# Reordering ScalarE and VectorE in a two-layer conditioned feed-forward kernel on one Trainium2 core

## The reference

```python
y = einsum('bij,bkj->bik', x, L0_cond_weight[itok_B_1_14])
h = layernorm(y, gamma, beta)
h = quant_rows(h) @ quant_rows(w1).T + b1      # scale = max|row| / 127
h = gelu(h)
h = quant_rows(h) @ quant_rows(w3).T + b3
x = x + h
```

## Time and profile before

| what | us |
|---|---|
| time, median of 3 runs | 810.48 |
| lowest and highest of them | 808.19, 811.26 |
| the profiled execution: time | 810.76 |
| its span, first to last instruction | 809.0 |
| TensorE busy | 740.0 |
| VectorE busy | 523.9 |
| ScalarE busy | 350.1 |
| GpSimd busy | 68.4 |

### The profile page before, as it was taken

The page is one execution under the profiler, slowest core; times in us unless marked ns, Lnnn a source line. Parts: engine busy times, 40 slices in busy tenths (PEclk is TensorE's granted clock), DMA queues, the critical chain, the costliest instruction groups (busy, mean ns, idle before and its releaser), DMA issues.

```text
span 809.0 us, 9935 instructions
## 1 busy us (share of the span) xinstructions
PE 740.0 (91%) x3128; PEld 471.7 (58%) x3128; DVE 523.9 (65%) x1911; ACT 350.1 (43%) x660; POOL 68.4 (8%) x40
## 2 busy tenths in 40 slices
PE   8988999999899999999999799998999995799927
PEld 4544544254444444444666688887878774467616
DVE  4548482426664929365775524225988988999985
ACT  1252633213624333341644635435344252599613
POOL 0002000202630203021004000000000000000000
PEclk9999999999999999999999999999999999799958
DMA  7959954213729443534032133032030328666306
GB/s 304 409 164 404 277 202 153 94 53 130 260 95 390 142 159 138 182 118 156 1 111 87 53 117 118 1 118 108 11 118 17 103 96 285 216 228 200 122 0 208
DMA packets 54278, 124.31 MB, mean 154 GB/s; under 512 B 8015, under 2 KB 33743, under 8 KB 48722
## 3 DMA queue, kind: packets, MB, share of 16 engines
q1 hardware_dynamic: 52930, 120.94, 42.8%
q10 hardware_dynamic: 1296, 2.74, 0.9%
HBM read 98.47 MB, written 25.19 MB: 153 GB/s over the span
## 4 chain that ended last, share of the span: by engine, by line
PE 61%; DVE 17%; ACT 8%; DMA 7%; issue 4%; SPq 1%; POOL 1%; ACTq 0%; DVEq 0%
PE PS L850 17%; PE PS L1021 13%; PE PS L910 13%; DMA stage<-w_dram 3%; DMA wscale_scratch<-wsc 3%; PE PS L899 2%; PE PS L1133 2%; PE PS L1127 2%; PE PS L1173 2%; DVE xp L1422 2%; PE PS L943 2%; PE PS L1055 2%; DVE kprod L1512 2%; PE PS L1142 1%; DVE ksum L1516 1%
## 5 line engine op out<-in xcount | busy, mean ns | idle before, releaser
L850 PE MATMUL PS<-w_raw,x_raw 128*128 128x512 f32 x512 | 230.2, 603 | 5.2 <-DMA w_raw<-cond_w_dram 2.2
L850 PEld LDWEIGHTS PS<-w_raw,x_raw 128*128 128x128 f32 x512 | 96.6, 194 | 116.1 <-issue 114.1
L1021 PE MATMUL PS<-w_hi,xT_hi 128*128 128x512 f32 x256 | 102.7, 401 | 0.0
L1021 PE MATMUL PS<-w_hi,xT_lo 128*128 128x512 f32 x256 | 100.1, 391 | 0.0
L1021 PE MATMUL PS<-w_lo,xT_hi 128*128 128x512 f32 x256 | 100.0, 391 | 0.0
L569 ACT ACTIVATE qT<-PS,round_c 128x512 bf16<-128x512 f32 x64 | 40.2, 679 | 86.5 <-PE PS L899 86.5
L1273 DVE SCALAR_TENSOR_TENSOR gbuf<-PS,lnst,vecs 128x512 f32<-128x512 f32 x32 | 23.9, 750 | 80.2 <-PE PS L910 80.1
L488 POOL TENSOR_TENSOR xres<-xres,vecs 128x1024 f32<-128x1024 f32 x16 | 43.2, 2718 | 305.5 <-DMA xres<-x_tok_dram 305.5
L1516 DVE TENSOR_REDUCE ksum<-kprod 128x16 f32<-128x64 f32 x392 | 66.3, 211 | 0.0
L910 PE MATMUL PS<-w3q,qT 128*128 128x512 bf16 x256 | 58.0, 379 | 6.7 <-ACT qT L569 6.7
L1340 DVE TENSOR_TENSOR xT_lo<-PS,xT_hi 128x512 fp32r<-128x512 f32 x32 | 20.5, 682 | 63.3 <-ACT xT_hi L629 63.2
(11 more groups left out here) (180 smaller groups left out, 1188.4 us busy)
## 6 DMA issues: line engine op xcount, KB each, us to landing
w_raw<-cond_w_dram SPq DMA_DIRECT2D x31, 1024.0 KB, 5.9
x_raw<-x_tr_dram SPq DMA_DIRECT2D x32, 256.0 KB, 6.7
stage<-w_dram SPq DMA_DIRECT2D x16, 512.0 KB, 12.6
xres<-x_tok_dram SPq DMA_DIRECT2D x8, 1024.0 KB, 9.2
x_scratch<-x1buf SPq DMA_DIRECT2D x16, 512.0 KB, 6.6
x1n<-x_scratch SPq DMA_DIRECT2D x16, 512.0 KB, 5.8
y_scratch<-y SPq DMA_DIRECT2D x16, 512.0 KB, 3.7
stage<-base_w_nat_dram SPq DMA_DIRECT2D x8, 512.0 KB, 13.0
```

The costliest lines, as they stand in the source:

```text
L850: mm = pe.matmul(PS[:, 2 * t + h, :], x_raw[pr][:, c, t * P:(t + 1) * P], w_raw[pr][:, c, h * H2:(h + 1) * H2], start=(pr == 0 and c == 0) ...
L1021: pe.matmul(PS[:, 2 * t + h, :], xx[:, c, t * P:(t + 1) * P], ws[c // 2][:, c % 2, h * H2:(h + 1) * H2], start=(c == 0 and xx is xT_hi and ...
```

## The change

Six edits. (1) In the last part of a step s below 7, ScalarE evacuates the GELU transposes of tile 0 (`evac_T(s - 1, 0, 3)`) before the GELU of tile 1, and no more at the head of the next step; the root of the next batch's tile 0 follows that GELU at once, before `quant2`. In the third step `evac_T(1, 0, 3)` stands behind `composites_1`; after step 1 it stands behind the GELU. (2) In `step_a` the evacuation of tile 1 (`evac_T(s - 2, 1, 3)`) moves in front of `ln_root(s - 1, 1)`, and `split_hi(2)` moves behind `quant1`. (3) On VectorE `centre` of the next batch's tile 0 stands in front of `range_w1` of tile 1. (4) On TensorE the block `l0(1, 2)` stands in front of the transposes of stage 12, which go to the T banks now; their evacuation stands behind `quant1(0, 1)`. (5) The waits for free banks follow. (6) `WARM` is 28, not 16.

```diff
--- before.py
+++ after.py
@@ -79,8 +79,8 @@
 
         PS = ctx.enter_context(nc.psum_tensor("PS", [P, 8, H2], F32))
         T_BANK, O_BANK, LL_BANK, LG_BANK = 4, 6, 6, 7
-        WARM = 16
-        IN_O = (1, 3, 5, 7, 9, 11, 12)
+        WARM = 28
+        IN_O = (1, 3, 5, 7, 9, 11)
 
         def stage_bank(m):
 
@@ -591,9 +591,9 @@
             evac_stage(KC + 3)
             quant1(0, 0)
             evac_T(0, 0, 1)
-            evac_stage(KC + 4)
             ln_root(0, 1)
             quant1(0, 1)
+            evac_stage(KC + 4)
             evac_T(0, 1, 1)
             gelu(0, 0)
             quant2(0, 0)
@@ -603,6 +603,7 @@
             evac_stage(KC + 6)
             evac_stage(KC + 7)
             gelu(0, 1)
+            evac_T(0, 0, 3)
             quant2(0, 1)
             act.dma_start(w24[:, :, :], head_w).then_inc(misc_ld, 16)
             act.dma_start(bcol[:, :], bias_col).then_inc(misc_ld, 16)
@@ -630,19 +631,15 @@
                                          PS[:, T_BANK + h, :].rearrange("p (c n) -> p c n", c=4), ACT.Copy).then_inc(xh_done, 1)
 
             def step_a(s):
-                if s == 3:
-                    composites_1()
-                ln_root(s - 1, 0)
-                evac_T(s - 2, 0, 3)
+                if s == 2:
+                    ln_root(s - 1, 0)
+                quant1(s - 1, 0)
                 if s == HALF:
                     split_hi(2)
-                quant1(s - 1, 0)
                 if s == 3:
                     composites_2()
-                    evac_T(s - 2, 1, 3)
+                evac_T(s - 2, 1, 3)
                 ln_root(s - 1, 1)
-                if s != 3:
-                    evac_T(s - 2, 1, 3)
                 quant1(s - 1, 1)
                 if s == HALF:
                     split_hi(3)
@@ -661,7 +658,16 @@
                 if s == NB - 1:
                     evac_xT(0, 1)
                     return
+                if s == 2:
+                    gelu(s - 1, 1)
+                    ln_root(s, 0)
+                    quant2(s - 1, 1)
+                    composites_1()
+                    evac_T(s - 1, 0, 3)
+                    return
+                evac_T(s - 1, 0, 3)
                 gelu(s - 1, 1)
+                ln_root(s, 0)
                 quant2(s - 1, 1)
 
             for s in range(2, NB):
@@ -855,8 +861,10 @@
             def stage_T(m):
                 pe.wait_ge(st_q, m + 1)
                 for h in range(2):
-                    if m <= KC + 4:
-                        wait(pe, st_ev, 2 * (m - (1 if m == KC + 4 else 2)) + h + 1)
+                    if m < KC + 4:
+                        wait(pe, st_ev, 2 * (m - 2) + h + 1)
+                    elif m == KC + 4:
+                        pe.wait_ge(e1_done, h + 1)
                     elif m == KC + 5:
                         pe.wait_ge(e1_done, 2 + h + 1)
                     else:
@@ -869,6 +877,8 @@
             def t_bank_free(s, t, which, h):
                 if which == 1 and s == 0 and t == 0:
                     pe.wait_ge(st_ev, 2 * (KC + 2) + h + 1)
+                elif which == 1 and s == 0:
+                    pe.wait_ge(st_ev, 2 * (KC + 4) + h + 1)
                 elif which == 3 and s == 0 and t == 0:
                     pe.wait_ge(st_ev, 2 * (KC + 7) + h + 1)
                 elif which == 3 and s == NB - 2 and t == 0:
@@ -884,7 +894,7 @@
                 if t == 1:
                     pe.wait_ge(o1_done if which == 1 else o3_done, 4 * s + h + 1)
                 elif which == 1 and s == 0:
-                    pe.wait_ge(st_ev, 2 * (KC + 4) + h + 1)
+                    pe.wait_ge(st_ev, 2 * (KC + 3) + h + 1)
                 elif which == 1:
                     wait(pe, o3_done, 4 * (s - 1) + 2 + h + 1)
                 else:
@@ -924,8 +934,8 @@
             stage_T(KC + 3)
             l0(1, 1)
             transposes(0, 0, 1)
+            l0(1, 2)
             stage_T(KC + 4)
-            l0(1, 2)
             product(0, 0, 1)
             transposes(0, 1, 1)
             l0(1, 3)
@@ -1342,7 +1352,9 @@
                                             xT_hi[:, 4 * h:4 * h + 4, t * P:(t + 1) * P], ALU.subtract).then_inc(xl_done, 1)
 
             def step_a(s):
-                layer_norm(s - 1, 0)
+                if s == 2:
+                    centre(s - 1, 0)
+                normalise(s - 1, 0)
                 if s == 2:
                     dve.wait_ge(swld, 32)
                 if s == 3:
@@ -1352,7 +1364,9 @@
                 finish_w3(s - 2, 1)
                 finish_w1(s - 1, 0)
                 if s < NB - 1:
-                    finish_w1(s - 1, 1)
+                    scale_w1(s - 1, 1)
+                    centre(s, 0)
+                    range_w1(s - 1, 1)
 
             for s in range(2, NB):
                 step_a(s)
```

## The result

| what | before | after |
|---|---|---|
| median of the first comparison (6 executions each) | 809.83 | 801.30 |
| lowest and highest of them | 807.63, 811.26 | 799.25, 803.79 |
| the profiled execution: time, span | 810.76, 809.0 | 803.07, 801.2 |
| all executions of this study: number, mean, median | 72, 809.3, 809.6 | 20, 802.9, 803.3 |

The ratio of the first comparison is 0.9899 (95% interval 0.9873 to 0.9926), that is 8.2 us faster. Two later comparisons of the same kernel gave 0.9915 (0.9884 to 0.9945) and 0.9921 (0.9894 to 0.9948), and the difference of the means over all executions is 6.4 us.

What follows compares the result with a forecast made beforehand. TensorE, busy 740.0 us, was taken as the bound. 810.76 less 2.4 (lead left after step 4) and 3.1 (steps 5 to 7) gave 805.3, forecast as 805.0 since the median is 0.28 lower; 8-in-10 range 802.0 to 808.3.

Steps and rivals of the forecast that it cites:

- steps 5 to 7: Evacuating ahead of GELU removes TensorE's wait at the w3 product: 1.04 us gained per step, 3.1 in all.
- The block in front of stage 12: In TensorE's first 100 us, the block fills a 3.11 us wait and takes 7.03, not 8.51: lead 3.2 us.
- Warming: Twelve more transposes at the start: up to 1.8 us won in the first block, counted as 0.
- the stages come with TensorE: Rival, chance 0.11: the warmed start also brings the transfer of 53.40 forward; the lead grows by 1.7 us, giving 803.3.
- Step 4: TensorE runs 5.6 us ahead, but then waits for inputs behind the split chain; a lead of 2.4 us remains.
- the clock falls in the handover: Rival, chance 0.16: behind the new input waits TensorE's clock drops; at block (4,3) this costs 1.5 us, giving 806.5.
- The slower rival: Rival, chance 0.05: centring behind both GpSimd additions delays tile 1's rounding in every step; TensorE waits 1.3 us; 812.8.

Runs made afterwards that it cites:

- both splits early: The changed kernel with split_hi(2) and split_hi(3) of step 4 brought forward on ScalarE; 0.9858 (797.0 us), repeated 0.9822 (795.8 us), of the kernel before.

## Why the prediction came out as it did

**The steps 5 to 7: right, and 0.5 small.** After, the first block of step 7 starts at 344.37, 44.79 us behind that of step 6; before, it started at 349.73, 45.99 behind it:

```profile
344.37 7.03 PE L856 MATMUL PS<-w_raw,x_raw 128*128 128x512 f32 x16
```

```profile
349.73 7.03 PE L850 MATMUL PS<-w_raw,x_raw 128*128 128x512 f32 x16
```

That is 1.20 each and not 1.04. The product's start had also lost the 0.16 by which TensorE's groups overlap when nothing stands between them. It repeats: from l0(5,0) to l0(7,3) the five traces with the old order of edits 1 to 3 take 126.78 us, the thirteen with the new order 123.15 or 123.16. That is 3.6 in every execution, where 3.1 was forecast.

**The block in front of stage 12: right.** Over three executions l0(2,0) starts at 97.6 before; over four at 94.3 after: 3.3, where 3.2 was forecast. Over all 18 traces it is 96.8 to 98.1 with the old order of stage 12 and 93.1 to 95.4 with the new, 3.0 apart in the means. Alone it measured 3.6.

**Warming: 0, as forecast.** Alone it gave nothing; with both splits early there is no difference either. With the block in front of stage 12, l0(2,0) starts at 94.2 in the mean of three traces with 16 transposes and at 94.4 in that of ten with 28. The rival "the stages come with TensorE", which the first profile of the changed kernel seemed to bear out (VectorE began that stage at 51.45 and not 53.40), is not borne out as a lead: the stage's transposes start at 53.7 to 55.9 with 28 and at 54.6 to 56.4 with 16, ranges that overlap, and nothing of it is left at l0(2,0).

**Step 4: the chain right, its sequel wrong.** Counted from the lead of 6.2 that TensorE in fact had in that profile, the working gives the third split's end at 221.5 (measured 221.19), the centring at 222.6 (222.27) and the last landing at 241.0 (241.81). The waits came out the other way round: 1.8 to 1.9 for l0(4,2), where 2.2 to 3.5 was forecast, and 2.7 to 3.9 for l0(4,3) in three of the four, where 1.5 was. The forecast had taken the slower of its two times for the first load (231.3); with the quicker one (230) it would have had 2.8 for the second wait.

But the rival "the clock falls in the handover", put at 0.16, happened in every one of the four traces, at 1.7 to 2.8 us. Of the three traces of before, two had one slow group in step 4 (the product above, and l0(4,3)), the first none. This is where the mechanism of the forecast failed: it took waits of 2.2 to 3.5 and 1.5 for harmless, because a product behind 2.37 had kept its speed, although in its own the first block took 8.80 behind a wait of 2.20. The third trace of before has the slow product behind that very wait of 2.37. In step 4 waits of 1.86, 1.96, 2.04, 2.07 and 2.66 were followed by slow blocks, and so were all of 3.6 and more; those of 1.63 to 1.82, of 1.90, 2.73 and 2.96 were not. So from 1.86 to 2.96 these runs show no length that is safe. From l0(4,0) to l0(5,0) the changed kernel takes 51.9 us in the mean and the kernel before 50.0: the handover costs 1.9, where 0.8 was forecast (a lead of 3.2 in, 2.4 out). At l0(5,0) the lead is 1.6 in the means, not 2.4.

**The sum, and the range.** The slow handover made the kernel slower than forecast, and so can't be why it measured faster. The lead at the last block of the first layer is 5.2 us in the means (383.6 to 378.4), with 5.5 forecast: the costlier handover and the larger gain of steps 5 to 7 nearly cancel, and that the total comes so near is luck. The rest of the 6.4 us lies in the second layer, where no list changes: from l0(7,3) to the end it takes 424.5 to 427.6 us in the traces before and 423.2 to 427.5 after. That has a place. Some 40 us behind l0(7,3) VectorE's bias addition and the last of GpSimd's residual additions start almost together. In the third trace of before GpSimd is 0.07 us ahead, and the addition takes 3.39 us; in the first it is 0.70 behind, and the addition takes 1.23 (x15 instead of x16: one record is missing):

```profile
422.93 5.68 POOL L488 TENSOR_TENSOR xres<-xres,vecs 128x1024 f32<-128x1024 f32 x2 [39.30 <-DMA xres<-x_tok_dram]
423.00 3.39 DVE L1277 TENSOR_TENSOR gbuf<-gbuf,vecs 128x1024 f32<-128x1024 f32 x1
...
428.93 3.40 PE L910 MATMUL PS<-w1q,qT 128*128 128x512 bf16 x15 [2.85 <-ACT qT L569]
```

```profile
424.76 1.23 DVE L1277 TENSOR_TENSOR gbuf<-gbuf,vecs 128x1024 f32<-128x1024 f32 x1
...
425.46 5.10 POOL L488 TENSOR_TENSOR xres<-xres,vecs 128x1024 f32<-128x1024 f32 x2 [40.18 <-DMA xres<-x_tok_dram]
...
428.29 3.63 PE L910 MATMUL PS<-w1q,qT 128*128 128x512 bf16 x16 [0.47 <-ACT qT L569]
```

In five of the 18 traces GpSimd is ahead, by 0.03 to 0.14 us; in the others it starts with VectorE or behind it. These five have a wait of 2.8 to 3.1 us there and a rest of 425.7 to 427.6, all others one of 0.5 to 0.7 and a rest of 422.4 to 424.5; in two of the five the product behind the wait is slow as well (4.6 and 5.1 us). It falls on two of the three traces of before and on one of the four after. Whether the change moves these odds, or this was chance, so few traces don't tell; with the old order of edits 1 to 3 it is two in five, with the new three in thirteen.

What put 801.3 outside the range was thus the last step of the working, from the sum to the range. The miss is 3.7 us, and it divides so: 1.2 for the base (810.48, a median of three, where the mean of 72 executions is 809.3), 1.2 for the second layer (the 6.4 less the 5.2 of the first), 1.6 because the six executions of the first comparison were quicker than the mean of all twenty (801.3 to 802.9), less the 0.3 by which the first layer gained less than forecast. None of the first three had a term: the range was built from the forecast's mechanisms alone, though single executions of one kernel differ by 7 us (799.25 to 806.68 in the changed one). By the ratio the forecast was 0.9932; all comparisons of the whole lie between 0.9899 and 0.9921, the first of them 2 us further than the parts add up to (6.1).

**The slower rival fell:** no trace has a wait of TensorE for the rounding of tile 1 in steps 5 to 7, with or without edit 3.

**A version that beats both** is the changed kernel with both splits early: 0.9822 and 0.9858 of before, 795.8 and 797.0 us.

## What to carry to other kernels

When a chain is moved, list what its engine does in front of the one instruction that another engine or a transfer waits for: the split that frees a buffer belongs into the first idle gap of its engine, even where it then holds up a neighbour that has slack. Price a new wait of about 2 us or more on TensorE with the fall of the clock behind it (1.7 us and up to 2.8 here), and expect that it comes in some executions and not in others. Take a forecast as a ratio to many executions of the kernel before, give its range a term for how far these lie apart, and look for blocks and waits in the profile that came by chance before using its times as a base. Compare traces by the time between two blocks of TensorE: with no wait between them it repeated to 0.01 us here, where whole executions differ by several.

## Of the hardware, not expected

The clock's falls are not reproducible: l0(3,1), behind the small matmuls of `composites_2`, took 8.83 us in some executions and 7.13 in others of the same kernel. With 16 warming transposes the first block took 8.80 in the four traces with a wait of 2.07 to 2.25 us ahead of it; behind waits of 1.79, 1.80 and 1.90 it took 7.11, 8.73 and 7.11. With 28, and at most 1.1 us of waiting, it took 7.03 to 7.11 in all eleven traces. The wait at 55 for a stage ends anywhere from 53.77 to 55.84 in four executions of the same kernel, and the fall of the clock that sometimes follows widens that: l0(1,1) starts at 55.57 and at 59.10. A start of 0.03 to 0.14 us earlier on GpSimd made a VectorE addition of 1.2 us last 3.4, and a wait of 0.5 to 0.7 us on TensorE 2.8 to 3.1. And the same transpose of the identity took 0.16 to 0.22 us at the start (4.58 to 6.14 for 28, in eleven traces) and 0.125 in step 4 (1.75 for 14).
